# Three attention stages: head loads issued before the maxima rows, vector work in ring order, and the reciprocal chain issued by POOL

## The reference

```python
x = x + L0(_gn(x))   # A: 12-head attention over 1024 tokens, rotary position (q, k times cos + rotated times sin)
x = x + L1(_gn(x))   # B: selective scan in four directions
x = x + L2(_gn(x))   # C: 12-head attention, scores plus relative row and column terms
x = x + L3(_gn(x))   # D: 12-head attention in a 7 x 7 neighbourhood
```

## Time and profile before

| | us |
|---|---|
| median of 3 runs | 8861.15 (8851.8 to 8868.71) |
| profiled execution | 8870.59 |
| its span, first to last instruction | 8868.8 |
| PE busy | 7117.3 (80%) |
| DVE busy | 5281.6 (60%) |
| ACT busy | 3280.4 (37%) |
| POOL busy | 1168.2 (13%) |
| PE granted clock, mean | 0.864 |

### The profile page before, as it was taken

One profiled execution on the slowest core, in us unless ns is written; L12 is line 12 of the kernel. 1 busy time (PEld: TensorE's weight loads), 2 busy tenths in 40 slices (PEclk: granted clock), 3 DMA queues, 4 the chain that ended last, 5 costly groups with the idle time before them and its releaser, 6 DMA issues. The chain is left out here.

```text
span 8868.8 us, 86314 instructions
## 1 busy us (share of the span) xinstructions
PE 7117.3 (80%) x32664; PEld 2841.9 (32%) x32664; DVE 5281.6 (60%) x5310; ACT 3280.4 (37%) x3610; POOL 1168.2 (13%) x468
## 2 busy tenths in 40 slices
PE   6888888867777777777779999999989996777776
PEld 2222222223223223233234343344333432333332
DVE  5777777757777767777765555555555553333333
ACT  2555555532323322322323343333433432222222
POOL 0000000014334334334320000000000000000000
PEclk9999999988878778778778999999989997888787
DMA  2111111100000000000001001111010101222221
GB/s 65 47 46 48 48 48 48 46 23 0 7 7 0 7 7 0 7 7 0 4 29 29 27 29 35 29 30 30 27 35 27 30 25 54 65 66 62 64 68 46
DMA packets 152812, 282.83 MB, mean 32 GB/s; under 512 B 46858, under 2 KB 53762, under 8 KB 152398
## 3 DMA queue, kind: packets, MB, share of 16 engines
q1 hardware_dynamic: 152398, 277.31, 10.8%
HBM read 165.34 MB, written 89.79 MB: 29 GB/s over the span
## 5 line engine op out<-in xcount | busy, mean ns | idle before, releaser
L927 DVE TENSOR_REDUCE mx<-ring 128x1 f32<-128x1024 f32 (+1 forms) x1920 | 2187.8, 1141 | 2536.0 <-PE ring L674 1255.0
L825 ACT ACTIVATE pt<-ring 128x1024 f32<-128x1024 f32 (+1 forms) x1920 | 1868.4, 981 | 2836.0 <-PE ring L700 1329.5
L724 PE MATMUL px<-pt,vo 128*32 128x512 f32 (+3 forms) x8064 | 1277.2, 616 | 9.5 <-ACT pt L825 9.3
L671 PE MATMUL ring<-kb,qb 96*128 96x512 bf16 x3072 | 1121.2, 407 | 203.0 <-DVE rq L912 96.2
L698 PE MATMUL ring<-qb,kb 99*128 99x512 bf16 x3072 | 1124.0, 408 | 161.7 <-DVE nb L947 67.9
L1533 POOL TENSOR_TENSOR hc<-hs,crep 128x1024 f32<-128x1024 f32 x384 | 979.7, 2551 | 1684.0 <-DVE hs L1489 1593.7
L1228 PE MATMUL ring<-duh,spread 96*128 96x512 f32 x1536 | 650.7, 537 | 362.0 <-DVE hs L1478 230.5
L1489 DVE TENSOR_TENSOR_SCAN hs<-ring,hs 128x1024 f32<-128x1024 f32 x384 | 874.5, 2277 | 2.1 <-ACT ring L1376 2.1
L700 PE MATMUL ring<-rq,hot 128*128 128x512 f32 x1536 | 865.5, 622 | 0.0
L674 PE MATMUL ring<-hot,rq 128*128 128x512 f32 x1536 | 856.6, 616 | 0.0
L1376 ACT ACTIVATE ring<-ring,arow 128x1024 f32<-128x1024 f32 x384 | 415.9, 1083 | 947.8 <-PE ring L1217 947.8
(11 more groups left out here) (169 smaller groups left out, 6792.5 us busy)
## 6 DMA issues: line engine op xcount, KB each, us to landing
qk_parts<-part SPq DMA_DIRECT2D x192, 192.0 KB, 2.4
qb<-qk_parts SPq DMA_DIRECT2D x192, 96.0 KB
kb<-qk_parts SPq DMA_DIRECT2D x192, 96.0 KB
ocm<-os SPq DMA_DIRECT2D x576, 32.0 KB
rb<-reciprocals SPq DMA_DIRECT2D x288, 64.0 KB, 2.5
qb<-qk_parts SPq DMA_DIRECT2D x192, 64.0 KB
kb<-qk_parts SPq DMA_DIRECT2D x192, 64.0 KB
qk_split<-hi SPq DMA_DIRECT2D x32, 384.0 KB, 3.5
```

The costliest lines, as they stand in the source:

```text
L671: last = nc.tensor.matmul(out[:, half], m.qb[u][0:BR, q], m.kb[u][0:BR, half], start=True, stop=L == "A")
L724: last = nc.tensor.matmul(m.px[32 * g:32 * g + 32, h % 2, lo - f * HF:hi - f * HF], m.vo[img % 2][:, t, VW * head:VW * head + VC], pt[:, l ...
L825: nc.scalar.activation(pt, ps, ACT.Exp, scale=1.0 if L == "C" else HD ** -0.5).then_inc(s.pt, 1)
L927: nc.vector.tensor_reduce(out, ps, AX.X, ALU.max).then_inc(s.mx_used, 1)
```

## The change

Six edits:

```diff
 agenda:
-            put(size * (img + 1) + behind["proj"] + c, "proj", img, c)
-        put(size * (img + 1) + behind["proj"] + 2, "leave", img)
+            put(size * (img + 1) + behind["proj"] + 2 * c, "proj", img, c)
+        put(size * (img + 1) + behind["proj"] + 3, "leave", img)
 attn_tensor, claim:
             elif old[0] == "maxima":
-                pe.wait_ge(a.nm, heads + old[1] + 1)
+                pe.wait_ge(a.mt_used, heads + old[1] + 1)
 attn_vector, turn:
+        if 4 * img + i:
+            dve.wait_ge(s.rotated, 4 * img + i)
 attn_vector, negated:
+        nc.vector.tensor_scalar(m.nr[:], mt, -1.0, None, ALU.mult).then_inc(a.mt_used, 1)
+        nc.vector.drain()
         if L == "D":
-            nc.vector.tensor_scalar(m.nm[:, 0, :], mt, -1.0, None, ALU.mult)
+            nc.vector.tensor_copy(m.nm[:, 0, :], m.nr[:])
             nc.vector.drain()
-            nc.vector.scalar_tensor_tensor(m.nm[:, 1, :], mt, -1.0, m.nm[:, 0, :].bitcast(F32),
-                                           ALU.mult, ALU.subtract).then_inc(a.nm, 1)
+            nc.vector.tensor_tensor(m.nm[:, 1, :], m.nr[:], m.nm[:, 0, :].bitcast(F32), ALU.subtract).then_inc(a.nm, 1)
...
 attn_vector, the loop of a turn:
     for n in turns_of(L, plan):
+        for kind, img, i in plan.get(n, []):
+            if kind == "sums":
+                norm_variance(nc, dve, m, m.ring[0:CP, slot[(kind, img, i)], 0:2 * NC], turns(L, img))
+            if kind == "turn":
+                turn(img, i)
+            if kind == "rest" and L == "C":
+                rest(img, i)
+            if kind == "low" and L == "D":
+                low(img, i)
+            if kind == "proj":
+                residual(img, i)
         if 0 <= n < total:
             scores(n)
...
 attn_pool, normal:
+        pool.wait_ge(a.rdn, NC * (images + img) + c + 1)
+        nc.gpsimd.dma_start(m.rd[c], m.rdn[c][:]).then_inc(a.rd_out, 16)
+        pool.wait_ge(a.rd_out, 16 * (NC * (images + img) + c + 1))
+        if c == 1:
+            pool.wait_ge(a.oc[0], images + img + 1)
+        elif images + img:
+            pool.wait_ge(a.oc[1], images + img)
+        for i in range(HC):
+            src = m.rd[c:c + 1, NT * i:NT * (i + 1), :].rearrange("c t n -> c (t n)").broadcast_to([HD, N])
+            nc.gpsimd.dma_start(m.rb[HD * i:HD * (i + 1), :], src).then_inc(a.rb_in, 16)
         pool.wait_ge(a.rb_in, BACK_IN * (NC * (images + img) + c + 1))
 attn_sync, the loop of a turn (back and spread are removed):
-        if maxima_ready(L, n):
-            maxima(n // steps - 1)
         h, left = divmod(n - lead, steps)
         if left == 0 and 1 <= h and h - 1 + NBUF < NH * B:
             sp.wait_ge(s.st_ps, steps * h)
             load(h - 1 + NBUF, jobs)
+        if maxima_ready(L, n):
+            maxima(n // steps - 1)
```

More of the change, by code:

```diff
@@ L136, in __init__ @@
         self.mt = sem("mt")
+        self.mt_used = sem("mt_used")
         self.nm = sem("nm")
@@ L934, in negated @@
         mt = m.ring[0:NT, slot[("maxima", h)], 0:P]
+        nc.vector.tensor_scalar(m.nr[:], mt, -1.0, None, ALU.mult).then_inc(a.mt_used, 1)
+        nc.vector.drain()
         if L == "D":
-            nc.vector.tensor_scalar(m.nm[:, 0, :], mt, -1.0, None, ALU.mult)
+            nc.vector.tensor_copy(m.nm[:, 0, :], m.nr[:])
             nc.vector.drain()
-            nc.vector.scalar_tensor_tensor(m.nm[:, 1, :], mt, -1.0, m.nm[:, 0, :].bitcast(F32),
-                                           ALU.mult, ALU.subtract).then_inc(a.nm, 1)
+            nc.vector.tensor_tensor(m.nm[:, 1, :], m.nr[:], m.nm[:, 0, :].bitcast(F32), ALU.subtract).then_inc(a.nm, 1)
         else:
-            nc.vector.tensor_scalar(m.nb[:, 0, :], mt, -1.0, None, ALU.mult)
+            nc.vector.tensor_copy(m.nb[:, 0, :], m.nr[:])
             nc.vector.drain()
-            nc.vector.scalar_tensor_tensor(m.nr[:], mt, -1.0, m.nb[:, 0, :], ALU.mult, ALU.subtract)
+            nc.vector.tensor_tensor(m.nr[:], m.nr[:], m.nb[:, 0, :], ALU.subtract)
             nc.vector.drain()
@@ L983, in attn_vector @@
                 norm_moments(nc, m, turns(L, img))
-            if kind == "sums":
-                norm_variance(nc, dve, m, m.ring[0:CP, slot[(kind, img, i)], 0:2 * NC], turns(L, img))
             if kind == "apply":
@@ L989, in attn_vector @@
                 norm_apply(nc, dve, m, m.x[img % 2], turns(L, img))
-            if kind == "turn":
-                turn(img, i)
             if kind == "sum":
                 total_of(img, i)
-            if kind == "rest":
+            if kind == "rest" and L == "A":
                 rest(img, i)
-            if kind == "low":
+            if kind == "low" and L != "D":
                 low(img, i)
@@ L999, in attn_vector @@
                 reciprocal(img, i)
-            if kind == "proj":
-                residual(img, i)
         for h, axis in relatives(L, n):
@@ L1118, in store @@
             sp.dma_start(m.ocm[HD * i:HD * (i + 1), c, f * HF:(f + 1) * HF], o).then_inc(a.o_in[h % 2], 16)
[L1120 to L1134, removed]
     jobs = 0
@@ L1144, in attn_sync @@
                         load(h, jobs)
[L1145 to L1148, removed]
             if kind == "leave":
```

## The result

Median of 4 runs: 8448.83 us (8437.92 to 8455.57), against 8864.93 (8851.8 to 8871.46) for the kernel before on the same chip. The ratio is 0.9534 [0.9521, 0.9548], 416 us less. The forecast was 8480.

The account below looks back on a forecast made before the run. It took D's PE idle time, mostly waiting for head loads in a loop through SP, as the place to gain. D 290, A 36 + 30, C 40, less 22 gave 374 off 8861: 8487, said as 8480; 8-in-10 range 8340 to 8680.

Parts of the forecast that it names:

- Loads ahead of maxima: D, SP's queue: issuing a head's load before the maxima rows saves 37.5 us an image, 290 us in all.
- The bound over two heads: D: the load loop through SP limits a pair of heads to 16.7 to 19.2 us; 17.5 was taken.
- the extra per image: D: 5 us for the image's store and load plus 3 us for traffic before a load, making 137.5 an image.
- Chain on POOL: Reciprocal write and broadcasts issued by POOL, 1 us each: 22 us cost in all, at images and attention stages' ends.
- Early release: DVE frees the maxima slot after its first operation: 0.43 us in each of 84 waits in A, 36 us.
- Ring order: DVE takes a turn's other units before the scores' reduce: saves 30 us in A and 40 in C.
- Projections two turns apart: Spacing an image's two projections two turns apart was said to add nothing.
- Signs: Expected: D near 1170 us, clock above 0.85, ks wait under 120, nb under 25, rs under 20, no rdn wait on SP.
- Rival 1: D: maxima rows land behind the load and PE stalls about 2 us a head, 190 us; 8670, chance 0.12.
- rival 2: POOL's issues cost 2 us or more and PE waits for ocn/ocm; about 8580, chance 0.08.
- rival 4: Slower: DVE's wait for nm_in in negated holds up DVE, PE and the next store; 8870 or more, chance 0.04.
- Rival 3: D: load not earlier in effect, SP held by store, parts and the image's store; 8750, chance 0.05.

Follow-up runs that it names:

- e10: Kernel after, with an image's two projections in successive turns again and the image's store a turn earlier; 8413.35 us, ratio 0.9513.
- e1: Kernel after, with SP's old order restored: maxima rows first, then the head's load; 8601.15 us, ratio 0.9710.
- e2: Kernel after, with the reciprocals' write and the broadcasts issued by SP again; 8522.26 us, ratio 0.9629.
- e3: Kernel after, with DVE's old order restored: the scores' reduce before the turn's other units; 8596.19 us, ratio 0.9707.
- e9: Kernel after, with the maxima edit wholly undone: DVE's old four operations, slot released at their end; 8497.15 us, ratio 0.9602.
- e5: Kernel before, with one edit: SP's load ahead of the maxima rows; 8725.30 us, ratio 0.9839.
- e12: Kernel before, with only D's head load cut into six DMAs of 16 rows; 8575.96 us, ratio 0.9693.
- e7: Kernel after, with D's head load as six DMAs of 16 rows, where two of four had 32; 8285.12 us, ratio 0.9349.

## Why the prediction was right, and where its terms were off

The direction, the mechanism and the total were right; that the total came so near was partly luck, since two errors cancelled. By stage, with the cost of POOL's issues booked where it falls: D 278 us predicted, 203 measured; A 62 and 130; C 36 and 73; 9 are B's scatter.

**Loads ahead of maxima: right, but too large.** D was to lose 290 us. The bound over two heads held: from 7819.13 to 7837.93 two plain heads take 18.80, others 18.0 to 19.5, where 17.5 was taken. One head of such a pair still stalls for 4 us, and its second turn still runs at the lower level (0.90 us at 7832.37, behind the stall of 4.21), which the 17.5 had counted only in part. What failed is the extra per image. An image's period is 152 us (POOL issues rdn at 7557.02, 7709.59 and 7861.73) and not 137.5. The turns around the image's store and load, SP after the change:

```profile
7741.83 0.58 SPq L389 DMA_DIRECT2D out<-x  x1
7746.49 0.32 SPq L383 DMA_DIRECT2D x<-x_C  x1
7746.91 1.15 SPq L1107 DMA_DIRECT2D qs<-qk_split  x2
```

```profile
7758.58 0.87 PE L668 MATMUL ring<-ks,qs 112*128 112x320 f32 x2 [12.26 <-DMA ks<-qk_split]
```

From the load's first issue to PE's start it is 11.67 us instead of 8.56, so the interval is 7758.58 - 7739.70 = 18.88 in place of the 6.7 + 5 that were taken: about 7 of the 15 us. SP issues the image's load only when the store has landed, 4.66 us later, and the head's load right behind it; e10, which puts both a turn earlier, has 12.98 us there. The other 8 lie in the heads with jobs and tokens and the one behind them, which had 3 us for part traffic; why these are longer was not tested. Of the 203 us, e1 gives 133 to the order, e2 gives 52 to the chain's leaving SP, e3 10 to the ring order and e9 3 to the release: 198 in all. The term held the first two.

**Chain on POOL: the cost too large, a gain missed.** 1 us for an issue was taken; it is 0.5 (POOL's rows under e2), and PE's wait for ocm grew by 7 us in the whole execution, where 22 were booked. The later landing of POOL's DMAs, for which a sentence of the prediction had an estimate of 0.8 us, is 1.9 us for the write and 0.3 for the broadcasts by the medians; with the longer issues the chain costs 1.0 to 2.1 us more at the stages' ends. The 22 us in A that e2 shows weren't in the prediction, which said of SP only that a head's store and maxima stand behind the chain in D.

**Early release: right in A.** 36 against e9's 31; by the ratios it is worth 60 in the whole kernel, where the term had nothing for C and D.

**Ring order: right in kind, too small.** 30 in A and 40 in C were predicted; e3 shows 74 and 51. The step that failed is the price in A: it was one row of rs waits, 27.6, "with the few for x". The list of A before has more of them:

```profile
PE ring L698 <- DVE rs L874: 18.1, 7, 2.6
PE ring L631 <- DVE x L970: 14.5, 7, 2.1
PE ring L698 <- DVE x L970: 9.8, 7, 1.4
```

With the 27.6 that makes 70 us of waits for rs and x, of which 7.2 are left after the change (e3 has 58). The slower matmuls after each stall were left out too, 28 us in A. "Projections two turns apart add nothing" missed what e10 shows in D.

**Signs.** The clock (0.86) was above its sign, loads went ahead of maxima (after the head's start 1.9 us earlier in one head of a pair, 6.4 in the other, where some 4 were forecast), SP has no wait for rdn, and nb and rs are gone. D at 1256 and the ks wait at 182.6 missed theirs (near 1170, under 120), though D stayed under the 1300 that would have refuted the forecast. Rival 1 fell, the maxima rows' line didn't change; so did rival 2, by POOL's issue rows, and rival 4. Rival 3 fell in size (e5 and e1 give the order 133 to 145 us in D), but what it named, SP held by the image's store, is there once an image. Of the load over two engines the prediction had the rule right and the use wrong. It took them for a danger to the maxima rows, while they were the largest thing left: the 6.3 us after the last issue are a term of the bound (8.56), and cutting the pieces to 16 rows (e12, e7) takes 4.2 of them. The rule of the Trainium skill ("DMA: Bandwidth & Descriptors", Why a DMA increments its semaphore by 16 and not by 1) is borne out by these two kernels: with a slowest dimension of 2 the load keeps 0.13 of the 16 engines busy, two of them, and with one of 16 the same bytes keep 0.46 busy and are used 2.1 us after the last issue.

The four undone edits (e1, e2, e3, e9) cost 453 us by the ratios and 363 by the profiled executions, on either side of the 416 that the change brought. A clear interaction between them isn't shown.

## What to carry to other kernels

Where PE stalls on a load in a loop through a queue, write the loop as a sum (what stands ahead of the load, its issue, its landing) and attack the largest term: here reordering the queue alone won 143 us (e5), and spreading the same bytes over more engines alone 272 (e12). Both together with the other edits (e7) are 6.5% under the kernel before, the best version found; e10's edit on top of it was not run. Release a shared slot after the first read of it, in the order in which its writer wants it back; and price a stall with the slower matmuls behind it, not by its length alone.

## What the runs showed of the hardware

Issuing the 24 KB write and one 64 KB broadcast took POOL 0.56 and 0.48 us, SP 0.42 and 0.44; they landed 3.3 and 2.8 us (median) after POOL's issue, 1.4 and 2.5 after SP's. A head's load of 384 KB on SP's queue was used 6.3 us after its last issue as four DMAs, two of them with 2 x 16 rows, and 2.1 us after it as six of 16 rows; the busy share of the DMA engines meanwhile was 0.13 (two of 16) and 0.46. The same four DMAs right behind the 768 KB load of an image took 3.1 us longer to PE's start (11.67 against 8.56). In the busy stage A, matmuls behind a stall of 2.07 us ran at a granted clock of 0.50 (1.04 us for the pair), behind one of 0.51 us at 1.00 (0.61).
